# Key matching over four columns in the last three iterations of a graph layer: one wait for four scatters

## The chip, the cores and the metric

One core of a Trainium2 chip runs the whole kernel. The metric is the device time of one execution in microseconds (us), the median over several.

## The reference

Two graph layers in a residual stream over N = 50000 nodes with D = 128 features and E = 25000 edges, sorted by destination. Layer 0 is graph attention. Layer 1, which the change touches, sends a message along each edge and adds it to the row of the edge's source node:

```python
h = jnp.maximum(_layernorm(x, axis=-1), 0.0)
row, col = src, dst                       # edge_index = stack([src, dst])
bond_weights = sigmoid(edge_attr @ Wa + ba)
messages = concatenate([h[row], h[col], edge_attr], axis=-1)
messages = relu(messages @ W1 + b1) @ W2 + b2
messages = messages * bond_weights
x = x + h + segment_sum(messages, row, num_segments=N)
```

## The kernel before

Edges lie in SBUF as 128 partitions by COLS = 196 columns; an edge is a partition and a column. Layer 1 takes G4 = 4 columns in an iteration, so there are ITS = 49 iterations (0 to 48), walked from the last columns to the first. The first four iterations and the last five (44 to 48) are written out, the others are a hardware loop over four at a time; `u` is the iteration modulo 4 and picks one of four buffers.

An iteration runs over four engines, and semaphores alone set the order between them:

- **POOL** issues the indirect transfers: the scatters (L1170), which add a column of 128 message rows to rows of the output in DRAM, and the gathers (L1156) of the source nodes' rows for three iterations ahead (FETCH = 3). An adding scatter reads a row, adds and writes it back, so two scatters that touch the same row must not be in flight together. POOL therefore treats the four columns of an iteration as two pairs: before each pair it waits until all earlier scatters have landed (`ms_add`), and between the pairs it issues gathers. In the last three iterations (46 to 48) there is nothing more to gather. Ahead of the first pair it also waits for the targets (`ms_sx`) and for the message rows UPD (`ms_upd`).
- **PE** transposes the rows of the destination (L1368), those gathered from the source (L1376), the keys (L1357, 128 source indices a column) and the edge features (L1360); multiplies by W1 (L1383, L1385, L1387) and W2 (L1392, L1395); and at last sums rows of equal key with one-hot matrices S2 (L1408). In one pair two edges may have the same source. Their rows are summed, the first of them carries the sum, and the others are sent to spare rows behind the N real ones.
- **DVE** scales the messages by the bond weights (L1269, into MS), and then, in `match`, prepares the next iteration's keys: for each column a compare of the transposed keys of its pair, 256 wide, with its own key, which gives the one-hot matrix S2 (L1250), and a masked count of equal keys that come earlier (L1253, 128 wide for the first and 256 wide for the second column of a pair); then four steps on 128x4 that give the scatter's targets `sx` (L1256 to L1261). Behind it comes `prepare` for three iterations ahead (L1213 to L1230), until iteration 45.
- **ACT** copies out of PSUM: the hidden layer (L1312), UPD (L1326) and the transposed rows (L1306, L1300, L1294).

PE's order in the written-out part of iteration `it` is: W1 of `it+1`, products L1408 of `it`, transposes L1368, L1376, L1357, L1360 of `it+2`, and W2 of `it+1`. Transposes of `it+2` and W1 of `it+1` end with iterations 46 and 47. So L1376 of iteration 48 stands ahead of W2 of iteration 47, and W2 ahead of the scaling and L1408 of iteration 47.

Of the kernel before, what the change touches and what calls it, by code (L numbers as in the profile page):

```python
# [19 lines left out]
ALU = mybir.AluOpType  # L20
# [3 lines left out]
P = 128  # L24
# [11 lines left out]
def gnn_program(nc, x, src, dst, bond, w_embed, a_src, a_dst, w_lin, bias0, w1, b1, w2, b2, wa, ba, out):  # L36
# [27 lines left out]
    with ctx:  # L64
# [103 lines left out]
        with nc.Block() as block:  # L168
# [49 lines left out]
            @block.gpsimd  # L218
            def _(pool):
                nc.gpsimd.memset(ones, 1.0).then_inc(tri_init, 1)  # L220
                pool.wait_ge(tri_init, 1)
                for t, pattern, mult, op in ((ident, [[-1, P]], 1, ALU.is_equal), (ltri[:, P:2 * P], [[-1, P]], 1, ALU.is_gt),
                                             (utri, [[1, P]], -1, ALU.is_gt)):
                    nc.gpsimd.affine_select(out=t[:, 0:P], in_=ones, compare_op=op, fill=0.0, base=0,
                                            pattern=pattern, channel_multiplier=mult).then_inc(consts, 1)
                nc.gpsimd.memset(ltri[:, 0:P], 1.0).then_inc(consts, 1)
                nc.gpsimd.iota(spare[:, :], [[0, 2], [2 * P, 2]], base=2 * N + 1, channel_multiplier=2,
                               allow_small_or_imprecise_dtypes=True).then_inc(consts, 1)
                nc.gpsimd.iota(lane, [[1, COLS]], base=0, channel_multiplier=0,
                               allow_small_or_imprecise_dtypes=True).then_inc(lanes_set, 1)  # L230
                pool.wait_ge(order_known, 1)
                with pool.If(pool.value_load(unsorted[0:1, 0:1]) > 0):
                    lim = pool.to_reg(P * COLS - 1)
                    pool.wait_ge(ranks_ready, 1)
                    pool.wait_ge(ld_unranked, 32)
                    pool.wait_ge(bond_rows, 16)
                    pool.wait_ge(bond_tail, 16)
                    with pool.Fori(0, COLS) as j:
                        nc.gpsimd.tensor_copy(rank1[:, :], rank[:, bass.ds(j, 1)]).then_inc(rank_copied, 1)
                        nc.gpsimd.tensor_copy(pair1[:, :], pairs[:, bass.ds(j, 1), :].rearrange("p o s -> p (o s)")).then_inc(rank_copied, 1)  # L240
                        nc.gpsimd.tensor_copy(bond1[:, :], H[:, bass.ds(j * BOND, BOND)]).then_inc(rank_copied, 1)
                        pool.wait_ge(rank_copied, 3 * j + 3)
                        pool.sem_inc(rank_go, 1)
                        pool.indirect_dma_start(ranked, bass.IndirectOffsetOnAxis(rank1[:, 0:1], 0), pair1[:, :], None,
                                                bounds_check=lim, oob_is_err=True).then_inc(ranked_out, 16)
                        pool.indirect_dma_start(bonds, bass.IndirectOffsetOnAxis(rank1[:, 0:1], 0), bond1[:, :], None,
                                                bounds_check=lim, oob_is_err=True).then_inc(ranked_out, 16)
                        pool.wait_ge(ranked_out, 32 * j + 32)
                        pool.sem_inc(rank_go, 1)
# [880 lines left out]
        cnt, tt, kcol, kdif = (Rw[:, 768 + 4 * n:772 + 4 * n] for n in range(4))  # L1130
        bprod = Rw[:, 1024:1024 + G4 * BOND]
        HDST = Rw[:, 1280:1280 + G4 * D]
        ld_s = [sem(f"ms_gathered{u}") for u in range(4)]
        (ms_keys, ms_bond, ms_flip, ms_hs, ms_bt, ms_hid, ms_hidr, ms_msg, ms_scaled, ms_sum, ms_upd, ms_go, ms_sgo,
         ms_sx, ms_chain, ms_col, ms_zb, ms_bw, ms_fill, ms_hd, ms_flipd, ms_add) = (sem("ms_" + n) for n in (
# [4 lines left out]
        with nc.Block() as block:  # L1140
# [10 lines left out]
            @block.gpsimd  # L1151
            def _(pool):
                lim = pool.to_reg(2 * ROWS_OUT - 1)

                def fetch(u, c):
                    pool.indirect_dma_start(XS4[u][:, c, :], None, halves, bass.IndirectOffsetOnAxis(ixs[:, u, c:c + 1], 0),  # L1156
                                            bounds_check=lim, oob_is_err=False).then_inc(ld_s[u], 16)

                def body(it, u, k):
                    more = upto(it, ITS - 1 - FETCH)  # L1160
                    f = (u + FETCH) % 4
                    for pair in range(2):
                        if pair == 0:
                            pool.wait_ge(ms_sx, it + 1)
                            pool.wait_ge(ms_upd, it + 1)
                        if past(k) or u or pair:
                            pool.wait_ge(ms_add, 32 * (2 * it + pair))  # L1167
                        pool.sem_inc(ms_sgo, 1)
                        for c in (2 * pair, 2 * pair + 1):
                            pool.indirect_dma_start(halves, bass.IndirectOffsetOnAxis(sx[:, u, c:c + 1], 0),  # L1170
                                                    UPD[u][:, c * D:(c + 1) * D], None,
                                                    bounds_check=lim, oob_is_err=True, compute_op=ALU.add).then_inc(ms_add, 16)
                        if more:
                            if pair == 0:
                                pool.wait_ge(ms_ix, it + FETCH + 1)  # L1175
                                if past(k) or u:
                                    pool.wait_ge(ms_flip, it)
                                pool.sem_inc(ms_go, 1)  # L1178
                            fetch(f, 2 * pair)
                            fetch(f, 2 * pair + 1)  # L1180
                for n in range(FETCH):
                    pool.wait_ge(ms_ix, n + 1)
                    for c in range(G4):
                        fetch(n, c)
                loop4(pool, body)
                pool.wait_ge(ms_add, 16 * COLS)

            @block.vector
            def _(dve):
# [42 lines left out]
                def prepare(it, u, k, base):  # L1232
                    fill(it, u, base)
                    weigh(it, u, k, base)

                def match(it, u, early, reused, base):
                    n = [0]

                    def link(ins):
                        n[0] += 1  # L1240
                        ins.then_inc(ms_chain, 1)
                        dve.wait_ge(ms_chain, base + n[0])
                    dve.wait_ge(ms_keys, it + 1)
                    if not early:
                        dve.wait_ge(ms_sum, it - 1)
                    q = blk(it)
                    for c in range(G4):
                        kc = key1[:, bass.ds(q * G4 + c, 1)]
                        p0 = c // 2 * 2 * P
                        nc.vector.tensor_scalar(S2[u % 2][:, c * 2 * P:(c + 1) * 2 * P], bK[u % 2][:, p0:p0 + 2 * P], kc, None, ALU.is_equal)  # L1250
                        w = (1 + c % 2) * P
                        j0 = c // 2 * 3 * P + c % 2 * P
                        nc.vector.scalar_tensor_tensor(junk[:, j0:j0 + w], bK[u % 2][:, p0:p0 + w], kc, ltri[:, 2 * P - w:2 * P],  # L1253
                                                       ALU.is_equal, ALU.mult, accum_out=cnt[:, c:c + 1])
                    k4 = key1[:, bass.ds(q * G4, G4)]
                    link(nc.vector.tensor_tensor(kdif, spare[:, :], k4, ALU.subtract))  # L1256
                    link(nc.vector.tensor_scalar(tt, cnt, 1.0, None, ALU.min))
                    link(nc.vector.tensor_tensor(tt, kdif, tt, ALU.mult))
                    if reused:
                        dve.wait_ge(ms_add, 16 * G4 * (it - 3))  # L1260
                    nc.vector.tensor_tensor(sx[:, u, :], tt, k4, ALU.add).then_inc(ms_sx, 1)  # L1261

                def body(it, u, k):
# [4 lines left out]
                    for c in range(G4):  # L1268
                        last = nc.vector.tensor_scalar(MS[:, c * D:(c + 1) * D], bM[:, c * D:(c + 1) * D], bwc[:, u % 2, c:c + 1],  # L1269
                                                       None, ALU.mult)  # L1270
                    last.then_inc(ms_scaled, 1)
                    if upto(it, ITS - 2):
                        match(it + 1, (u + 1) % 4, not (past(k) or u), past(k) or u == 3, base)
                    if upto(it, ITS - 4):
# [73 lines left out]
            def _(pe):  # L1348
# [50 lines left out]
                def body(it, u, k):  # L1399
# [3 lines left out]
                    if past(k) or u:  # L1403
                        pe.wait_ge(ms_upd, it)
                    pe.wait_ge(ms_sx, it + 1)
                    for c in range(G4):
                        for b in (c // 2 * 2, c // 2 * 2 + 1):
                            last = nc.tensor.matmul(bU[:, c * D:(c + 1) * D], S2[u % 2][:, (2 * b + c % 2) * P:(2 * b + c % 2 + 1) * P],  # L1408
                                                    MS[:, b * D:(b + 1) * D], start=(b % 2 == 0), stop=(b % 2 == 1), skip_group_check=True)
                    last.then_inc(ms_sum, 1)  # L1410
                    if upto(it, ITS - 3):
                        k2 = k + (u >= 2)
# [38 lines left out]
```

## Time and profile before

| what | us |
|---|---|
| median of 3 runs | 1546.91 (1546.25 to 1549.86) |
| the profiled execution, its time | 1547.89 |
| its span, first to last instruction | 1546.1 |
| layer 1's first gather to last scatter issued | 872.5 to 1540.3 |
| an iteration of layer 1 in the loop | about 13.3 |
| iterations 46, 47, 48 on POOL, first scatter | 1507.07, 1519.11, 1531.09 |
| POOL busy, share of the span | 1138.5, 74% |
| mean granted TensorE clock | 0.873 |

The profile gives busy times of each engine, and for an instruction the idle time of its engine just before it with what ended it. A scatter is busy on POOL only while POOL writes its descriptors; the transfer itself goes on behind it, until it lands. The span counts from the first to the last instruction, so the execution's time lies 1.8 us above it.

### The profile page before, as it was taken

Reading aid. Unit: us, or ns where it says so; the run is one execution under the profiler, and the core shown is the slowest. Engines: PE = TensorE matmul, PEld = TensorE weight load, DVE = VectorE, ACT = ScalarE, POOL = GpSimd, SP = SyncE. Lnnn points to the kernel's source line nnn. Section 1 sums busy time; section 2 is a strip of 40 time slices with the busy share of each in tenths; the row PEclk is TensorE's granted clock in tenths of the full one; section 3 lists DMA queues with packets and bytes.
Section 4 is the critical chain, followed back from the end, with each engine's and each line's share of the span. In section 5 each row is a group of like instructions: output and inputs, shape, how many; then the busy total and the mean of one; then the engine's idle time right before and its main releaser. Section 6 shows DMA issues by size and latency. Waiting matters only on the chain. (4 is left out here: it accounts for less than half of the span.)

```text
span 1546.1 us, 26048 instructions
## 1 busy us (share of the span) xinstructions
PE 1014.0 (66%) x5651; PEld 752.9 (49%) x5651; DVE 1102.4 (71%) x3786; ACT 780.6 (50%) x2168; POOL 1138.5 (74%) x992
## 2 busy tenths in 40 slices
PE   0777777777777754555554376777776767676773
PEld 0655555555555534545554154545454444444542
DVE  2989888898988988888889455565565656555551
ACT  0788888888888885656655122222222222222220
POOL 5777777777777704777776568888888888888884
PEclk9989999999999987787777589888898989888897
DMA  8477776777777654555554223333333333333322
GB/s 272 126 216 214 217 226 212 230 210 219 216 215 229 212 172 140 177 174 179 178 172 139 74 41 50 52 49 49 49 51 49 51 49 49 47 50 49 51 40 22
DMA packets 177765, 201.77 MB, mean 131 GB/s; under 512 B 22219, under 2 KB 130767, under 8 KB 177599
## 3 DMA queue, kind: packets, MB, share of 16 engines
q1 hardware_dynamic: 119421, 122.80, 24.8%
q0 software_dynamic: 56496, 71.62, 23.2%
q10 hardware_dynamic: 1810, 6.93, 1.4%
q8 instruction: 13, 0.21, 0.1%
q14 instruction: 25, 0.20, 0.0%
HBM read 90.62 MB, written 109.84 MB: 130 GB/s over the span
## 5 line engine op out<-in xcount | busy, mean ns | idle before, releaser
L1113 POOL DMA_INDIRECT out_dram<-BD,sx x196 | 201.1, 1026 | 118.0 <-issue 63.4
L1156 POOL DMA_INDIRECT XE<-out_dram,ixs x196 | 211.5, 1079 | 70.0 <-issue 53.8
L1269 DVE TENSOR_SCALAR XN<-bank,bwc 128x128 f32<-128x128 f32 x196 | 55.2, 344 | 243.4 <-PE bank L1395 236.0
L710 ACT ACTIVATE BD<-BD,nmr,rstd 128x128 f32<-128x128 f32 x392 | 171.1, 490 | 67.7 <-DVE nmr L571 67.7
L1170 POOL DMA_INDIRECT out_dram<-BS,sx x100 | 160.8, 1608 | 44.2 <-issue 37.9
L1052 PE MATMUL bank<-BD 128*128 128x128 f32 x392 | 105.6, 363 | 119.9 <-DVE BD L933 119.9
L1170 POOL DMA_INDIRECT out_dram<-TS,sx x96 | 153.6, 1600 | 38.1 <-issue 30.2
L1376 PE MATMUL bank<-ident,XE 128*128 128x128 f32 x196 | 42.1, 352 | 184.9 <-DMA XE<-out_dram,ixs 184.9
L773 PE MATMUL bank<-ident,BD 128*128 128x128 f32 x588 | 108.0, 295 | 80.0 <-DVE BD L564 78.9
L785 PE MATMUL bank<-wes,TS 128*128 128x132 f32 x392 | 100.4, 339 | 72.3 <-ACT TS L721 68.9
L1052 PEld LDWEIGHTS bank<-BD 128*128 128x128 f32 x392 | 82.8, 261 | 130.0 <-issue 130.0
L1312 ACT ACTIVATE XN<-bank,b1c 128x512 f32<-128x512 f32 x49 | 33.7, 687 | 207.7 <-PE bank L1387 207.7
L1300 ACT COPY XN<-bank 128x512 f32<-128x512 f32 x49 | 28.7, 586 | 192.6 <-PE bank L1376 192.6
L787 PE MATMUL bank<-wls,TS 128*128 128x128 f32 x784 | 124.8, 284 | 0.0
L435 POOL DMA_INDIRECT XE<-in_x_dram,ix x96 | 100.9, 1051 | 29.3 <-issue 25.9
L1376 PEld LDWEIGHTS bank<-ident,XE 128*128 128x128 f32 x196 | 26.7, 172 | 196.3 <-DMA XE<-out_dram,ixs 196.3
L785 PEld LDWEIGHTS bank<-wes,TS 128*128 128x128 f32 x392 | 60.8, 195 | 118.3 <-ACT TS L721 107.0
L721 ACT ACTIVATE TS<-bank 128x512 f32<-128x512 f32 x196 | 114.4, 584 | 1.4 <-DVE nmr L571 0.7
L773 PEld LDWEIGHTS bank<-ident,BD 128*128 128x128 f32 x588 | 66.6, 147 | 99.2 <-DVE BD L564 93.6
L435 POOL DMA_INDIRECT R<-in_x_dram,ix x88 | 92.0, 1045 | 26.8 <-issue 24.1
L435 POOL DMA_INDIRECT XN<-in_x_dram,ix x88 | 92.0, 1045 | 26.8 <-issue 23.5
L435 POOL DMA_INDIRECT O<-in_x_dram,ix x88 | 91.4, 1039 | 26.8 <-issue 23.5
(229 smaller groups left out, 3236.5 us busy)
## 6 DMA issues: line engine op xcount, KB each, us to landing
out_dram<-BD SPq DMA_DIRECT2D x98, 512.0 KB, 3.0
base_rows<-BD SPq DMA_DIRECT2D x49, 256.0 KB, 3.7
BD<-base_rows SPq DMA_DIRECT2D x49, 256.0 KB, 3.2
H<-BD SPq DMA_DIRECT2D x49, 256.0 KB, 2.8
XE<-in_x_dram SPq DMA_DIRECT2D x13, 512.0 KB
BD<-bond_rows SPq DMA_DIRECT2D x49, 128.0 KB, 2.1
bond_rows<-in_edge_attr_dram ACTq DMA_DIRECT2D x1, 6250.0 KB, 23.9
XN<-in_x_dram SPq DMA_DIRECT2D x12, 512.0 KB, 6.2
```

Of the source, the lines that this page charges most:

```text
L435: pool.indirect_dma_start(XA[u][:, c, SRC - s, :], None, x, bass.IndirectOffsetOnAxis(at, 0), bounds_check=lim, oob_is_err=False).then_inc ...
L710: last = nc.scalar.activation(OT[u][:, g, w:w + D], OT[u][:, g, w + D:w + 2 * D], ACT.Relu, bias=nmr[:, slot, t:t + 1], scale=rstd[:, slot ...
L721: nc.scalar.activation(TS[:, g % 2, :], psT[g % 2][:, :], ACT.Relu).then_inc(ts_ready, 1)
L773: last = nc.tensor.transpose(psT[g % 2][:, q * D:(q + 1) * D], t, ident[:, :])
L785: nc.tensor.matmul(a[:, 0:D + HEADS], t[:, SRC * D:(SRC + 1) * D], wes[:, :], start=True, stop=True, skip_group_check=True)
L787: nc.tensor.matmul(b[:, r * D:(r + 1) * D], t[:, r * D:(r + 1) * D], wls[:, 0:D], start=False, stop=False, skip_group_check=True)
L1052: nc.tensor.matmul(ps[6][:, 0:D], DG[u][:, c, :], BS4[u][:, c, :], start=first, stop=final, skip_group_check=True)
L1113: pool.indirect_dma_start(out, bass.IndirectOffsetOnAxis(sx[:, u, c:c + 1], 0), RO4[u][:, c, :], None, bounds_check=lim, oob_is_err=False) ...
L1156: pool.indirect_dma_start(XS4[u][:, c, :], None, halves, bass.IndirectOffsetOnAxis(ixs[:, u, c:c + 1], 0), bounds_check=lim, oob_is_err=Fa ...
L1170: pool.indirect_dma_start(halves, bass.IndirectOffsetOnAxis(sx[:, u, c:c + 1], 0), UPD[u][:, c * D:(c + 1) * D], None, bounds_check=lim, o ...
L1269: last = nc.vector.tensor_scalar(MS[:, c * D:(c + 1) * D], bM[:, c * D:(c + 1) * D], bwc[:, u % 2, c:c + 1], None, ALU.mult)
L1376: last = nc.tensor.transpose(bS[:, c * D:(c + 1) * D], XS4[u % 4][:, c, :], ident[:, :])
```

## The change

In iterations 46, 47 and 48 (`WIDE` = 46) equal keys are matched over all four columns of the iteration instead of over pairs. Each compare is 512 wide, the counts are 128, 256, 384 and 512 wide, with a mask `upto4` that is put together once in iteration 44. The one-hot matrices S4 and the other buffers lie in columns of H that layer 1 has already used up. L1408 becomes 16 products instead of 8. POOL leaves out the wait ahead of the second pair in these iterations, so that the four scatters follow one wait. The table of spare rows has four different ranges of rows instead of two; it is used in all iterations.

```diff
-                nc.gpsimd.iota(spare[:, :], [[0, 2], [2 * P, 2]], base=2 * N + 1, channel_multiplier=2,
+                nc.gpsimd.iota(spare[:, :], [[2 * P, G4]], base=2 * N + 1, channel_multiplier=2,
...
+        WIDE = ITS - FETCH
+        S4 = [H[:, 8192 + n * 2048:10240 + n * 2048] for n in range(2)]
+        junk4, upto4 = H[:, 12288:14336], H[:, 14336:14336 + G4 * P]
...
-                        if past(k) or u or pair:
+                        wide = isinstance(it, int) and it >= WIDE
+                        if (past(k) or u or pair) and not (wide and pair):
                             pool.wait_ge(ms_add, 32 * (2 * it + pair))
...
+                def wide_keys(it, u):
+                    for c in range(G4):
+                        kc = key1[:, bass.ds(blk(it) * G4 + c, 1)]
+                        w = (1 + c) * P
+                        nc.vector.tensor_scalar(S4[it % 2][:, c * G4 * P:(c + 1) * G4 * P], bK[u % 2][:, :], kc, None, ALU.is_equal)
+                        nc.vector.scalar_tensor_tensor(junk4[:, c * G4 * P:c * G4 * P + w], bK[u % 2][:, 0:w], kc, upto4[:, G4 * P - w:],
+                                                       ALU.is_equal, ALU.mult, accum_out=cnt[:, c:c + 1])
...
+                    if isinstance(it, int) and it >= WIDE:
+                        wide_keys(it, u)
+                    else:
+                        pair_keys(it, u)
...
+                    if isinstance(it, int) and it == WIDE - 2:
+                        nc.vector.tensor_copy(upto4[:, 0:P], ltri[:, 0:P])
+                        nc.vector.tensor_copy(upto4[:, P:2 * P], ltri[:, 0:P])
+                        nc.vector.tensor_copy(upto4[:, 2 * P:4 * P], ltri[:, :])
...
+                    wide = isinstance(it, int) and it >= WIDE
                     for c in range(G4):
-                        for b in (c // 2 * 2, c // 2 * 2 + 1):
-                            last = nc.tensor.matmul(bU[:, c * D:(c + 1) * D], S2[u % 2][:, (2 * b + c % 2) * P:(2 * b + c % 2 + 1) * P],
-                                                    MS[:, b * D:(b + 1) * D], start=(b % 2 == 0), stop=(b % 2 == 1), skip_group_check=True)
+                        for b in range(G4) if wide else (c // 2 * 2, c // 2 * 2 + 1):
+                            hot = S4[it % 2][:, (G4 * b + c) * P:(G4 * b + c + 1) * P] if wide else \
+                                S2[u % 2][:, (2 * b + c % 2) * P:(2 * b + c % 2 + 1) * P]
+                            last = nc.tensor.matmul(bU[:, c * D:(c + 1) * D], hot, MS[:, b * D:(b + 1) * D],
+                                                    start=(b == 0 if wide else b % 2 == 0), stop=(b == G4 - 1 if wide else b % 2 == 1),
+                                                    skip_group_check=True)
```

`pair_keys` holds the compares and counts of before, unchanged.

## Rows read from the trace of the kernel before

**Rows 1.** The chain of waits from 1400 us on, shares by line.
```profile
by line: POOL out_dram L1170 35.1%; issue 28.5%; POOL XE L1156 13.5%; DMA out_dram<-TS,sx 8.9%; DMA out_dram<-BS,sx 6.5%; DMA XE<-out_dram,ixs 1.8%; PE bank L1376 0.5%; POOLq L1178 0.2%; POOLq L1168 0.2%; POOLq L1167 0.1%; POOLq L408 0.1%; 
```

**Rows 2.** The same chain in order of time: start us, us, what.
```profile
1509.00 3.26 DMA out_dram<-TS,sx
...
1514.92 3.30 DMA out_dram<-TS,sx
```

**Rows 3.** POOL's timeline: start us, us, instruction, idle before it and its releaser.
```profile
1505.73 1.03 POOL L1156 DMA_INDIRECT XE<-out_dram,ixs  x1 [0.31 <-issue]
1507.07 1.62 POOL L1170 DMA_INDIRECT out_dram<-TS,sx  x1 [0.30 <-issue]
...
1513.05 1.57 POOL L1170 DMA_INDIRECT out_dram<-TS,sx  x1 [2.49 <-DMA out_dram<-TS,sx]
...
1519.11 1.55 POOL L1170 DMA_INDIRECT out_dram<-TS,sx  x1 [2.62 <-DMA out_dram<-TS,sx]
1520.96 1.55 POOL L1170 DMA_INDIRECT out_dram<-TS,sx  x1 [0.30 <-issue]
...
1526.88 1.55 POOL L1170 DMA_INDIRECT out_dram<-TS,sx  x1 [0.31 <-issue]
1531.09 1.55 POOL L1170 DMA_INDIRECT out_dram<-BS,sx  x1 [2.66 <-DMA out_dram<-TS,sx]
...
1538.77 1.55 POOL L1170 DMA_INDIRECT out_dram<-BS,sx  x1 [0.30 <-issue]
```

**Rows 4.** Landing times of L1170, from 1518 us on, then from 1200 us on.
```profile
DMA to landing us min/median/max: 3.2/3.3/3.4
...
DMA to landing us min/median/max: 3.2/3.3/4.3
```

**Rows 5.** PE's timeline, iterations 46 and 47.
```profile
1502.59 1.95 PE L1408 MATMUL bank<-XN,O 128*128 128x128 f32 x16
1504.38 0.60 PE L1368 MATMUL bank<-ident,BD 128*128 128x128 f32 x4
1508.33 0.66 PE L1376 MATMUL bank<-ident,XE 128*128 128x128 f32 x4 [3.35 <-DMA XE<-out_dram,ixs]
...
1515.63 1.95 PE L1408 MATMUL bank<-XN,O 128*128 128x128 f32 x16
1517.51 0.39 PE L1392 MATMUL bank<-b,on 3*128 3x512 bf16 x1
```

**Rows 6.** ACT's copies of the sums out of PSUM, iterations 47 and 48.
```profile
1517.61 0.58 ACT L1326 COPY TS<-bank 128x512 f32<-128x512 f32 x1 [0.91 <-PE bank L1408]
...
1522.29 0.59 ACT L1326 COPY BS<-bank 128x512 f32<-128x512 f32 x1 [4.09 <-DMA out_dram<-TS,sx]
```

**Rows 7.** Timelines of ACT, POOL and PE, iterations 43 and 44.
```profile
1466.07 0.58 ACT L1326 COPY TS<-bank 128x512 f32<-128x512 f32 x1 [0.91 <-PE bank L1408]
...
1467.66 1.66 POOL L1170 DMA_INDIRECT out_dram<-TS,sx  x1 [0.76 <-issue]
...
1468.51 0.66 PE L1376 MATMUL bank<-ident,XE 128*128 128x128 f32 x4 [2.12 <-DMA XE<-out_dram,ixs]
...
1474.26 1.95 PE L1408 MATMUL bank<-XN,O 128*128 128x128 f32 x16
```

**Rows 8.** PE by stretches: us, busy (count), granted clock, DMA share, GB/s.
```profile
1509.00:1510.50 1.50, 1.50 (x9) 0.59 0.50 44
```

**Rows 9.** DVE's timeline, the scalings of 45 and 48 and match 47.
```profile
1486.58 0.61 DVE L1269 TENSOR_SCALAR XN<-bank,bwc 128x128 f32<-128x128 f32 x2 [7.33 <-PE bank L1395]
...
1501.26 0.34 DVE L1253 SCALAR_TENSOR_TENSOR R<-bank,key,ltri 128x128 f32<-128x128 f32 x1
1501.53 0.48 DVE L1250 TENSOR_SCALAR O<-bank,key 128x256 f32<-128x256 f32 x1
1501.92 0.48 DVE L1253 SCALAR_TENSOR_TENSOR R<-bank,key,ltri 128x256 f32<-128x256 f32 x1
...
1519.02 1.12 DVE L1269 TENSOR_SCALAR XN<-bank,bwc 128x128 f32<-128x128 f32 x4 [1.45 <-PE bank L1395]
```

More of the change, by code:

```diff
@@ L1234, in prepare, with pair_keys @@
                     weigh(it, u, k, base)
+                def wide_keys(it, u):
[5 more added lines that the diff above has]
+                                                       ALU.is_equal, ALU.mult, accum_out=cnt[:, c:c + 1])
+                def pair_keys(it, u):
+                    for c in range(G4):
+                        kc = key1[:, bass.ds(blk(it) * G4 + c, 1)]
+                        p0 = c // 2 * 2 * P
+                        nc.vector.tensor_scalar(S2[u % 2][:, c * 2 * P:(c + 1) * 2 * P], bK[u % 2][:, p0:p0 + 2 * P], kc, None, ALU.is_equal)
+                        w = (1 + c % 2) * P
+                        j0 = c // 2 * 3 * P + c % 2 * P
+                        nc.vector.scalar_tensor_tensor(junk[:, j0:j0 + w], bK[u % 2][:, p0:p0 + w], kc, ltri[:, 2 * P - w:2 * P],
+                                                       ALU.is_equal, ALU.mult, accum_out=cnt[:, c:c + 1])
                 def match(it, u, early, reused, base):
@@ L1245, in match @@
                         dve.wait_ge(ms_sum, it - 1)
+                    if isinstance(it, int) and it >= WIDE:
+                        wide_keys(it, u)
+                    else:
+                        pair_keys(it, u)
                     q = blk(it)
[L1247 to L1254, printed above, removed]
                     k4 = key1[:, bass.ds(q * G4, G4)]
```

## The prediction

> **What bounds the kernel now.** I read the chain of waits of the last 147 us first. Its shares by line say that the layer-1 scatter (L1170) and the gather (L1156), both issued by POOL, carry it, with the scatters' transfers behind them [rows 1]. Up to 1507 us POOL never waits long: it issues scatter, scatter, gather, gather, with 0.30 us between them, and every wait on an earlier scatter is covered by the gathers. From iteration 46 on there is nothing left to gather. In order of time the chain then shows what remains uncovered: 3.26 and 3.30 us from a scatter's issue until it lands, and POOL issues again only about 0.8 us after that [rows 2, 3]. POOL's timeline gives the period exactly. Inside a pair the second scatter starts 1.85 to 1.93 us after the first; between pairs the start moves by 4.05 us in an iteration (1509.00 to 1513.05) and by 4.2 us from one iteration to the next (1526.88 to 1531.09), where POOL passes three waits instead of one [rows 2, 3]. A landing costs 3.2 to 3.4 us in this stretch [rows 4].
>
> So there are five uncovered waits behind the six pairs. The change takes three of them away (inside iterations 46, 47 and 48) and leaves the two between iterations. What has to be asked is what else a group of four waits for, and that is UPD: POOL also waits until ACT has copied the sum out of PSUM (L1326), which follows the one-hot products (L1408) on PE.
>
> **Part 1: three waits go.** Before, the third scatter of an iteration starts about 4.05 us after the second; after, it starts 1.87 us after it. This gives 4.05 - 1.87 = 2.18 us each, 6.5 us in all, if POOL alone set the pace. That is the most that the change can give.
>
> **Part 2: the products double.** L1408 now multiplies four blocks into each of four columns, 16 products for 8; PE shows each as two matmuls, so x32 for x16. From the start of L1408 to the next work on PE are 1504.38 - 1502.59 = 1.79 us for the x16 at full clock [rows 5]; the second x16 adds as much. Nearer zero would need PE to have had room in those 1.79 us, but the matmuls stand back to back; at half clock it would be up to 3.6 us, and this is the upper bound. I take 1.79. The path here is PE, ACT's copy, POOL, so it counts in full wherever UPD is awaited.
>
> How long from the copy to POOL: in iteration 43 the copy ends at 1466.07 + 0.58 = 1466.65 and POOL, idle before, starts at 1467.66, 1.01 us later [rows 7]. In iteration 47 of before the copy ends at 1517.61 + 0.58 = 1518.19 [rows 6] and POOL starts at 1519.11 [rows 3], 0.92 us later. So there the copy and the landing (1514.92 + 4.2 = 1519.1, rows 2) allow the same start: iteration 47 has no slack for its UPD already. That is the place where the gain is lost.
>
> **Iteration 46.** Its copy starts 1.98 us after L1408 (1517.61 - 1515.63, rows 5 and 6), so 1502.59 + 1.98 + 1.79 = 1506.36; end 1506.94, POOL at 1507.95 for 1507.07. The four scatters start at 1507.95, 1509.88, 1511.75 and 1513.62, and by the landing alone iteration 47 could start at 1513.62 + 4.19 = 1517.8.
>
> **Iteration 47.** Its messages hang on the last gather, issued at 1505.73, before any scatter that moves, and landed at 1508.33, when PE goes on (L1376) [rows 3, 5]. The products of iteration 46 and the transposes L1368 behind them now end at 1504.98 + 1.79 = 1506.8 and are still out of the way. But PE then idles 1.6 us before L1376 where it idled 3.35. In before the granted clock falls to half at about 1509.3, after these 3.35 us (0.59 is the mean of 1509.00 to 1510.50) [rows 8], and L1376 to L1408 takes 1515.63 - 1508.33 = 7.30 us [rows 5]. In iteration 44, after an idle stretch of 2.12 us, the same work ran faster: 1474.26 - 1468.51 = 5.75 us [rows 7]. With 1.6 us idle I take 5.75, the value of the row with the shorter idling, and 7.30 as the bound. Then L1408 starts at 1514.08, the copy at 1514.08 + 1.98 + 1.79 = 1517.85, ends 1518.43, and POOL starts at 1519.44. This is later than the landing allows (1517.8) and 0.3 us later than before: all that iteration 46 saved is lost here.
>
> A rule of the Trainium skill bears on this ("TensorE: Matmul & The Clock Gate", Part 1: The HAM clock gate): the gate's default is the slow state, activity releases it, and the point at which it switches differs from run to run for one kernel. By the trace, the stretch after 2.12 us of idling runs in its shorter time, and the sum is the one above; by the page's remark on runs a fall could still come at another place, and the sum would be that of the second rival.
>
> **Iterations 47 and 48.** Four scatters: 1519.44 + 3 x 1.85 = 1525.0; landing and waits 4.21: iteration 48 starts at 1529.2 for 1531.09. UPD of 48 is in time: L1392 follows L1408 of 47 at 1.88 + 1.79 = 3.67 after its start, the scaling (L1269) 1.51 later (1519.02 - 1517.51) [rows 5, 9], at 1519.3; from it to the copy 3.27 us before (1522.29 - 1519.02) [rows 6, 9], 5.06 now, so the copy ends at 1524.9 and POOL could start at 1525.9, 3.3 us before it is asked. The last scatter of all starts at 1529.2 + 5.55 = 1534.8 for 1538.77: **4.0 us** earlier. Nothing behind it changes.
>
> **Part 3: DVE.** Steps of DVE from start to start: 0.27 us for 128 columns (1501.26 to 1501.53), 0.39 for 256 (1501.53 to 1501.92) [rows 9], so some 0.13 for each further 128. Wide: four compares of 512 (0.65 each) and counts of 128, 256, 384 and 512 (0.27, 0.39, 0.52, 0.65), 4.43 us; before 6 x 0.39 + 2 x 0.27 = 2.88. So 1.55 us more in each of three matches (nothing as the lower bound, 2.9 if all doubled). It is covered: match 48 ended 1.45 us before the last scaling, that is 1.94 after the start of L1408 of 47; now at 3.49, and the scaling comes at 5.18: slack 1.7. Match 47, running at 1501 and now over by about 1506.1, is due at L1408 of 47, 1514.1, and match 46 as long before its own. If the cover were gone, each us late in match 48 would first use up that 1.7 and the 3.3 of UPD 48. The three copies of masks in iteration 44, 128x128 twice and 128x256 once, cost between nothing and 0.27 + 0.27 + 0.39 = 0.93 us by the same steps; DVE idles 7.33 us before the next scaling, at 1486.58 [rows 9], so nothing.
>
> **Part 4: the table of spare rows** now differs over four columns in all iterations. Only which rows the few duplicates go to changes; instruction and bytes stay: nothing.
>
> **The sum.** 4.0 us off this execution's own 1547.9 (span 1546.1, 1.8 around it) gives 1543.9; the median of the runs shown is 1546.91, 1.0 lower, and the prediction is made against that: **1542.9 us**, 0.26% less. The measurement tells about 0.3%, 4.6 us, from nothing, so this lands just inside "no change".
>
> **Rivals.**
> - *Nothing takes over.* POOL alone sets the pace, UPD 47 is in time: 6.5 us, 1540.4. It needs UPD 47 some 2.5 us earlier than worked out. For it only the bound; against it the row in which copy and landing already tie. 0.10.
> - *The clock falls again* in the stretch before UPD 47. Then 7.30 for 5.75: start of 47 at 1521.0, gain 2.4, 1544.5. For it the row of before; against it the shorter idling. 0.15.
> - *The fourth scatter lands later* since four read-modify-write transfers follow one another: the loop shows landings up to 4.3 us [rows 4]. One us more, in 47 and in 48, leaves 2.0: 1544.9. Against it: at most two are in flight at a spacing of 1.87 us and 3.3 us each, as in a pair now. 0.10.
> - *The other side, slower*: the same mechanism grown to a queue. X us more per landing cost 2X, and X - 1.6 more once iteration 46's slack (1519.4 - 1517.8) is gone. From 1.9 us more (5.2 for 3.3) nothing is gained; from 3.4 more (6.7) it is slower by 0.3%, about 1551.5. No landing in the tail is over 3.4. 0.03.
> - The forecast: 0.62. It spreads by about 1 us for the measurement and for 0.86 to 1.01 us from copy to POOL.
>
> **How the numbers follow.** The range goes from the first rival's 1540.4 to 1545.6, past the third's 1544.9 by what the runs scatter; about 0.15 is left out. Within the forecast somewhat more than a third lies beyond 4.6 us: 0.62 x 0.38 = 0.24, with the first rival 0.10: faster 0.34. Slower 0.03. Same 0.63. The first kernel's runs reach up to 1549.86, which says that single ones can be 3 us off.
>
> **What would show it.** After: in iterations 46 to 48 L1170 x4 with 0.30 us between; POOL's wait before 47 put down to ACT or PE, or a landing that was over 1.5 us before; L1408 x32 in 3.7 us; L1376 to L1408 in about 5.75 us at clock 1.00; UPD 48 ready 3 us early; the last scatter about 5.55 us after the first of 48. I am wrong if POOL's wait before 47 is 2.6 us again (then 46 was worth its 2 us), if the clock shows 0.5 before 1512, or if landings exceed 3.4.

## The result and the profile after

The changed kernel takes 1545.26 us (median of 22 runs, 1541.37 to 1548.92); the first kernel beside it 1547.89 (22 runs, 1541.81 to 1552.44). The ratio is 0.9982, with a 95% interval of 0.9974 to 0.9991: 2.8 us faster, between 1.4 and 4.0. Forecast were 4.0 us less and a time of 1542.9. The interval lies wholly below 1, so the change makes the kernel faster, by less than the 0.3% that the prediction called "no change". The measured time lies 2.4 us above the forecast one: 1.0 of them because the first kernel itself has a median of 1547.89 here and had 1546.91 in the three runs that the forecast started from, 1.4 because the gain between the medians is 2.6 us and not 4.0.

POOL's timeline of the changed kernel (start us, us, instruction, idle before it and its releaser; L1160 is the gather, L1175 the scatter) answers to [rows 3]:

```profile
1506.99 1.04 POOL L1160 DMA_INDIRECT XE<-out_dram,ixs  x1 [0.30 <-issue]
1508.88 1.62 POOL L1175 DMA_INDIRECT out_dram<-TS,sx  x1 [0.84 <-ACT TS L1349]
1510.81 1.57 POOL L1175 DMA_INDIRECT out_dram<-TS,sx  x1 [0.31 <-issue]
1512.68 1.57 POOL L1175 DMA_INDIRECT out_dram<-TS,sx  x1 [0.31 <-issue]
1514.56 1.56 POOL L1175 DMA_INDIRECT out_dram<-TS,sx  x1 [0.30 <-issue]
1520.56 1.55 POOL L1175 DMA_INDIRECT out_dram<-TS,sx  x1 [4.44 <-ACT TS L1349]
...
1526.14 1.55 POOL L1175 DMA_INDIRECT out_dram<-TS,sx  x1 [0.30 <-issue]
1530.36 1.55 POOL L1175 DMA_INDIRECT out_dram<-BS,sx  x1 [2.66 <-DMA out_dram<-TS,sx]
...
1535.93 1.55 POOL L1175 DMA_INDIRECT out_dram<-BS,sx  x1 [0.30 <-issue]
```

The waits inside the iterations are gone. But the wait ahead of iteration 47 has grown from 2.62 us to 4.44, and its releaser is no longer a transfer but ACT's copy of UPD.

The last gather of this execution comes 1.26 us later than in the trace of before (1506.99 for 1505.73); the scatter of the stretch ahead of it is shown at the end of the section on the prediction. So I count from there: **G is the start of the last gather**, and everything the change touches on the path lies behind it. Times after G, in us:

| start of | before | predicted | after |
|---|---|---|---|
| iteration 46 | 1.34 | 2.22 | 1.89 |
| iteration 47 | 13.38 | 13.71 | 13.57 |
| iteration 48 | 25.36 | 23.5 | 23.37 |
| the last scatter | 33.04 | 29.1 | 28.94 |

The tail is 4.1 us shorter, forecast 4.0. PE and ACT in the same stretch (L1399 the transposes of the gathered rows, L1434 the products, L1349 the copy into UPD) answer to [rows 5, 6]:

```profile
1503.67 3.73 PE L1434 MATMUL bank<-XN,H 128*128 128x128 f32 x32
1507.44 0.59 ACT L1349 COPY TS<-bank 128x512 f32<-128x512 f32 x1 [2.70 <-PE bank L1434]
1509.67 0.66 PE L1399 MATMUL bank<-ident,XE 128*128 128x128 f32 x4 [1.83 <-DMA XE<-out_dram,ixs]
1515.41 3.73 PE L1434 MATMUL bank<-XN,H 128*128 128x128 f32 x32
1519.18 0.59 ACT L1349 COPY TS<-bank 128x512 f32<-128x512 f32 x1 [2.70 <-PE bank L1434]
1525.64 0.59 ACT L1349 COPY BS<-bank 128x512 f32<-128x512 f32 x1 [5.88 <-DMA out_dram<-TS,sx]
```

The products take 3.73 us for 1.95, 1.78 more. PE idles 1.83 us before L1399 instead of 3.35, and from L1399 to L1434 are 5.74 us instead of 7.30. The stretches view of PE (us, busy, granted clock, DMA share, GB/s) shows the difference, and answers to [rows 8]:

```profile
1509.50:1511.00 1.50, 1.33 (x12) 1.00 0.00 0
1511.00:1512.50 1.50, 1.50 (x12) 1.00 0.52 44
1512.50:1514.00 1.50, 1.50 (x5) 1.00 0.50 44
```

The granted clock is 1.00, the level of 2.4 GHz, in all three stretches; in [rows 8] the mean was 0.59. The chain of waits in order of time shows the new path, from the last gather over PE and ACT to iteration 47:

```profile
1506.99 2.63 DMA XE<-out_dram,ixs
1509.67 0.66 PE bank L1399 x4
...
1515.58 3.58 PE bank L1434 x32
1519.18 0.59 ACT TS L1349
1519.81 0.76 issue
...
1526.14 3.33 DMA out_dram<-TS,sx
```

In [rows 1] PE had 0.5% of the chain from 1400 us on; the same view of the changed kernel gives its lines over 6%.

### The profile page after: what moved, and what is told of

Read it like the earlier page. It is cut to its first block and busy times, and to the rows that moved or that the text cites. A ratio compares the mean times of both kernels' runs of the same rounds, so it can differ in the third digit from the quotient of the medians.

```text
span 1543.3 us, 26147 instructions
## 1 busy us (share of the span) xinstructions
PE 1021.3 (66%) x5699; PEld 760.3 (49%) x5699; DVE 1107.9 (72%) x3789; ACT 781.3 (51%) x2168; POOL 1138.5 (74%) x992
## 5 line engine op out<-in xcount | busy, mean ns | idle before, releaser
L1160 POOL DMA_INDIRECT XE<-out_dram,ixs x196 | 211.7, 1080 | 69.8 <-issue 57.6
L1175 POOL DMA_INDIRECT out_dram<-BS,sx x100 | 160.7, 1607 | 43.6 <-issue 39.7
L1175 POOL DMA_INDIRECT out_dram<-TS,sx x96 | 153.6, 1600 | 35.2 <-issue 29.6
L1399 PE MATMUL bank<-ident,XE 128*128 128x128 f32 x196 | 41.4, 347 | 182.7 <-DMA XE<-out_dram,ixs 182.7
L1399 PEld LDWEIGHTS bank<-ident,XE 128*128 128x128 f32 x196 | 26.4, 170 | 194.0 <-DMA XE<-out_dram,ixs 194.0
L435 POOL DMA_INDIRECT XN<-in_x_dram,ix x88 | 91.9, 1044 | 26.8 <-issue 23.5
L435 POOL DMA_INDIRECT O<-in_x_dram,ix x88 | 91.4, 1039 | 26.8 <-issue 23.5
```

The costliest lines, as they stand in the source:

```text
L435: pool.indirect_dma_start(XA[u][:, c, SRC - s, :], None, x, bass.IndirectOffsetOnAxis(at, 0), bounds_check=lim, oob_is_err=False).then_inc ...
L1399: last = nc.tensor.transpose(bS[:, c * D:(c + 1) * D], XS4[u % 4][:, c, :], ident[:, :])
```

## The experiments

The theory: of the three waits, the one in iteration 46 is worth nothing, since iteration 47 starts when UPD 47 is there; the doubled products delay that; the waits in 47 and 48 are worth their 2.2 us each, less what the start of 47 loses. The rival: the start of 47 hangs on the transfers, or the change costs something elsewhere. All tails below are read as above, from G to the start of the last scatter, each from one trace. Two traces of the changed kernel agree in it to 0.1 us (28.94 and 28.89).

Experiments 1 and 2 and the first runs of 3 and 4 were made on a chip on which the first kernel takes 1744.44 us (median of 35 runs). No trace of the first kernel was taken there, but with only the table changed the tail is 33.11 us, for 33.04. The second runs of 4 and experiments 5 and 6 have 1546.88 us beside them, the second run of 3 and experiments 7, 8 and 9 have 1548.36 (medians of 23 runs of the first kernel). Experiments 5 to 8 are one execution each, of 1545.5 to 1546.4 us: single times scatter by more than what they are to tell apart, so only their tails are used.

**1. Only the table of spare rows.**
```diff
-                nc.gpsimd.iota(spare[:, :], [[0, 2], [2 * P, 2]], base=2 * N + 1, channel_multiplier=2,
+                nc.gpsimd.iota(spare[:, :], [[2 * P, G4]], base=2 * N + 1, channel_multiplier=2,
```


> The first kernel with only the new table of spare rows. Measured in the trace from the start of the last gather (G) to the start of the last scatter: 33.04 us in the first kernel, 28.94 us in the changed one. Theory (the table costs nothing, and the 1.3 us by which the changed kernel's last gather comes later is scatter of runs): 33.0 us after G, ratio of times 1.000. Rival (the table's other spare rows slow the transfers or something ahead of layer 1): ratio about 1.001, G about 1.2 us later than in the first kernel.

Tail 33.11 us, ratio 0.9994 (0.9979 to 1.0009): the table costs nothing in the tail, and nothing that the times can tell.

**2. Wide matching, but with the waits.**
```diff
-                        if (past(k) or u or pair) and not (wide and pair):
+                        if past(k) or u or pair:
                             pool.wait_ge(ms_add, 32 * (2 * it + pair))
```


> The changed kernel with the wait ahead of the second pair put back in iterations 46 to 48, so that only the cost of wide matching is left. Theory (the products delay UPD by 1.8 us, which shows where UPD is awaited): iteration 46 starts at G + 1.9 us for 1.34, iteration 47 is then set by the landing at G + 13.9, iteration 48 at G + 25.9, the last scatter at G + 33.6: 0.55 us slower than the first kernel, ratio 1.0004. Rival (wide matching costs nothing on the path): G + 33.0. Rival (DVE's longer match counts too): G + 35 or more.

Iterations 46, 47 and 48 start at G + 2.04, 14.22 and 26.21, the last scatter at 34.00; ratio 1.0010 (1.0000 to 1.0021). The cost of wide matching alone is 0.9 us in the tail, more than the 0.55 expected. Most of it comes from the start of 46, which is 0.7 us later; the starts of 47 and 48 are 0.8 and 0.9 later, and the last scatter 0.9 beside experiment 1:

```profile
1703.30 1.04 POOL L1160 DMA_INDIRECT XE<-out_dram,ixs  x1 [0.30 <-issue]
1705.34 1.62 POOL L1175 DMA_INDIRECT out_dram<-TS,sx  x1 [1.00 <-issue]
...
1717.52 1.55 POOL L1175 DMA_INDIRECT out_dram<-TS,sx  x1 [2.68 <-DMA out_dram<-TS,sx]
```

It is POOL's timeline of that kernel. The 2 us or more of the rival in which DVE's longer match counts do not appear.

**3. Wide only in iterations 47 and 48** (twice).
```diff
-        WIDE = ITS - FETCH
+        WIDE = ITS - 2
```


> Wide only in iterations 47 and 48. Theory (iteration 46's saved wait is worth nothing, since UPD 47 sets the start of 47): iteration 46 at G + 1.34, its PE idles 3.35 us before L1376 as in the first kernel. If the clock keeps its full level in the stretch behind that, iteration 47 starts at G + 13.7 and the last scatter at G + 29.0, as good as with three; if it falls as in the first kernel's trace, 15.3 and 30.6. Rival (each wait taken away is worth its 2.18 us): the last scatter at G + 31.1 or 28.9 + 2.2.

> Wide in 47 and 48 once more. PE idles about 3.4 us ahead of the transposes of the gathered rows. Theory (whether the clock falls behind this is luck of the run): L1399 to L1434 takes 5.75 us at full clock or 7.3 with a fall, iteration 47 starts at G + 13.7 or 15.1, the last scatter at G + 29.0 or 30.4. Over the runs the ratio lies at 0.9978 (3.4 of 1547 us), between the change's and one with 2.7 us. Rival: ratio 0.997, as the first time, which the tail cannot explain.

Iteration 47 starts at G + 15.11 and in the second run at 15.19, the last scatter at 30.42 and 30.49. In both traces PE idled 3.6 us before L1399 and its clock then fell. The second one's stretches:

```profile
1509.00:1510.50 1.50, 1.40 (x8) 0.66 0.45 38
1510.50:1512.00 1.50, 1.50 (x7) 0.50 0.26 14
1512.00:1513.50 1.50, 1.50 (x10) 0.71 0.32 35
```

L1399 to L1434 takes 7.31 us in both, and the start of 47 (15.1) is the one expected for a fallen clock. So the tail is 2.6 us shorter than before. The ratio was 0.9971 both times (0.9958 and 0.9959 to 0.9983), 5.1 and 4.5 us: more than the tail accounts for (the intervals begin at 3.0 and 2.6), and the rival of the second expectation is right on that number. More on it below.

**4. UPD in halves** (twice, the second time beside the changed kernel). In iterations 47 and 48 the sums of columns 2 and 3 go to a PSUM bank that is free by then, ACT copies columns 0 and 1 as soon as they are summed, and POOL waits for the other half only ahead of the third scatter (`halved(it)` is `it >= WIDE + 1`).
```diff
+                            if halved(it):
+                                pool.wait_ge(ms_updh, it - WIDE)
...
+                        elif halved(it):
+                            pool.wait_ge(ms_upd, it + 1)
...
+                        act.wait_ge(ms_half, it - WIDE)
...
+                        nc.scalar.copy(UPD[u][:, 0:2 * D], bU[:, 0:2 * D]).then_inc(ms_updh, 1)
+                        act.wait_ge(ms_sum, it + 1)
+                        nc.scalar.copy(UPD[u][:, 2 * D:4 * D], bD[:, 2 * D:4 * D]).then_inc(ms_upd, 1)
```


> The changed kernel, but in iterations 47 and 48 the sum of columns 2 and 3 goes to another PSUM bank, ACT copies columns 0 and 1 as soon as they are summed, and POOL waits for the second half only ahead of the third scatter. Theory (the second half of the products is what delays the start of 47): 47 starts at G + 11.8 for 13.57, where the landing of 46 and the half copy tie; the last scatter at G + 27.1 for 28.94; 5.9 us off the first kernel's tail, ratio about 0.9963. Rival (the start of 47 is set by the transfers): 47 at G + 13.5 and the last at G + 28.9, ratio as the change's 0.998.

> The changed kernel itself beside the next one. Theory: tail from G to the last scatter 28.9 us if PE keeps its full clock behind the last gather, ratio 0.9976 (4.1 of about 1744 us) within the scatter. Rival (the change costs 1 to 1.5 us ahead of the tail as well): ratio 0.9984.

> The kernel with half copies once more, beside the changed kernel on one chip. Theory: the tail is 1.8 us shorter than the changed kernel's (27.1 us from G), so the median is 1.8 us lower within the scatter of about 1 us, ratio to the first kernel 0.9966. Rival (something that the tail does not show takes the 1.8 us back): no difference between the two medians.

Iteration 47 starts at G + 11.79 and 12.09, the last scatter at 27.10 and 27.42, 5.9 and 5.6 us before the first kernel's. The changed kernel beside the second run: 13.59 and 28.89, as in its first trace. ACT's timeline of the second run, iteration 47 (L1359 copies the first half, L1361 the second):

```profile
1515.40 0.37 ACT L1359 COPY TS<-bank 128x256 f32<-128x256 f32 x1 [0.91 <-PE bank L1451]
1517.19 0.37 ACT L1361 COPY TS<-bank 128x256 f32<-128x256 f32 x1 [1.41 <-PE bank L1451]
```

and POOL, the fourth scatter of 46 and the first of 47:

```profile
1512.86 1.56 POOL L1185 DMA_INDIRECT out_dram<-TS,sx  x1 [0.30 <-issue]
1517.12 1.55 POOL L1185 DMA_INDIRECT out_dram<-TS,sx  x1 [2.70 <-DVE sx L1290]
```

The first half is there at 1515.77, 1.35 us before POOL starts, so now the landing sets the start: 4.26 us after the fourth scatter, as between iterations before. The releaser that the view names is not the right one. This write of `sx` ended just before, at 1516.96, but it holds the targets of iteration 48, and POOL waits at 47 only for those of 47, which were written at 1505.52. In the first run the view names the landing, 4.10 us after the fourth scatter:

```profile
1712.37 1.55 POOL L1185 DMA_INDIRECT out_dram<-TS,sx  x1 [2.54 <-DMA out_dram<-TS,sx]
```

Times: 0.9985 (0.9972 to 0.9998) on the first chip, 0.9971 (0.9959 to 0.9982) beside the changed kernel's 0.9979 (0.9968 to 0.9990) on the second; medians 1541.77 and 1543.63, for 1546.88. The 1.86 us between the two medians are the 1.8 expected, and drawing the twelve times of each kernel anew many times leaves 0.5 to 3.4 us between them. On the first chip the expected 0.9963 did not come: it lies outside the interval, and the median there (1740.63) is no lower than that of experiment 3 (1740.41), whose tail is 3.3 us longer. It is the fastest of the kernels by its tail.

**5. The products of iteration 47 twice.** The sums are the same; the second round starts anew.
```diff
-                    for c in range(G4):
+                    for c in [*range(G4)] * (2 if isinstance(it, int) and it == ITS - 2 else 1):
```


> The changed kernel with the 16 products of iteration 47 multiplied twice (the sums are the same), which adds about 3.6 us on PE there. G is the start of the last gather. Theory (the start of iteration 47 hangs on PE through UPD): it moves with the whole addition, from G + 13.6 to G + 17.1, and the last scatter from G + 28.9 to G + 32.5. Rival (the landing of iteration 46 sets it): nothing moves up to the first 1.6 us, or at all.

L1434 takes 7.31 us, and POOL's wait before 47 is:
```profile
1511.71 1.56 POOL L1175 DMA_INDIRECT out_dram<-TS,sx  x1 [0.31 <-issue]
1521.05 1.55 POOL L1175 DMA_INDIRECT out_dram<-TS,sx  x1 [7.78 <-ACT TS L1349]
```
With G at 1503.89 the start of 47 is at G + 17.16 (expected 17.1), the last scatter at G + 32.53 (32.5). Every us on PE there is a us of the tail.

**6. The products of iteration 48 twice.** The same edit with `it == ITS - 1`.

> The changed kernel with the 16 products of iteration 48 multiplied twice, 3.6 us more on PE. Theory (UPD 48 is ready about 3.1 us before the landing of 47 lets iteration 48 start): nearly all of it is covered, iteration 48 starts at G + 23.8 for 23.4 and the last scatter at G + 29.4 for 28.9. Rival (PE counts in each wide iteration): the last scatter at G + 32.5.

The copy of UPD 48 starts at 1529.20, with G at 1506.91, which is 3.6 us later after G than in the changed kernel, and POOL:
```profile
1526.11 1.55 POOL L1175 DMA_INDIRECT out_dram<-TS,sx  x1 [0.30 <-issue]
1530.58 1.55 POOL L1175 DMA_INDIRECT out_dram<-BS,sx  x1 [2.91 <-ACT BS L1349]
```
Iteration 48 starts at G + 23.67, the last scatter at 29.24: of 3.6 us more, 0.3 show. The slack of UPD 48 is therefore about 3.3 us, the number of the prediction.

**7. The products of iteration 46 twice.** The same edit with `it == ITS - 3`.

> The changed kernel with the 16 products of iteration 46 multiplied twice. Theory: UPD 46 comes 3.6 us later, iteration 46 starts at G + 5.5 for 1.9, its landing then sets 47 at G + 15.3 for 13.6 (iteration 46 has about 1.8 us of slack, the rest counts; PE reaches L1399, the transpose of the gathered rows, 1.5 us late, which would give 15.1), the last scatter at G + 30.6 for 28.9. Rival (46 counts in full): G + 32.5.

The last scatter is at G + 28.76, so nothing at all is lost, less than I had expected. Here L1434 of 46 began at 1502.75, 5.25 us before G (1508.00), and in the changed kernel's trace 3.32 before it (1503.67 and 1506.99), so iteration 46 started at 3.52 and not at 5.5. Its landing allowed G + 13.4 (9.20 + 4.2), and PE set it at 13.47. Iteration 46 has slack in the changed kernel, and its size goes with when PE gets there.

**8. Wide only in iteration 48**, `WIDE = ITS - 1`.

> Wide only in iteration 48. Theory (UPD 48 has 3 us of slack, so this one wait is worth its whole 2.18 us, and 47 starts as in the first kernel): iteration 47 at G + 13.4, 48 at G + 25.4, the last scatter at G + 30.9. Rival (each wide iteration pays 1.8 us on PE): the last scatter at G + 32.7.

Last scatter at G + 31.92, expected 30.9. From the start of 48 to the last scatter are 5.58 us for 7.68 before, 2.1 less: the wait is worth what was expected. What is missing is ahead of it: PE idled 4.99 us before L1399, and its granted clock was 0.50 from there to 1512,

```profile
1507.71 1.11 PE L1399 MATMUL bank<-ident,XE 128*128 128x128 f32 x4 [4.99 <-DMA XE<-out_dram,ixs]
...
1515.95 1.95 PE L1434 MATMUL bank<-XN,O 128*128 128x128 f32 x16
```

that is 8.24 us from L1399 to L1434, and iteration 47, with narrow products as in the first kernel, started at G + 14.28 for 13.38. UPD 47 can thus set the start even without wide products, when the clock is low.

**9. Wide in 47 and 48, and the eight products of 46 twice**: more work on PE ahead of the gathered rows. Beside the edit of experiment 3:
```diff
-                    for c in range(G4):
+                    for c in [*range(G4)] * (2 if isinstance(it, int) and it == WIDE - 1 else 1):
```


> Wide in 47 and 48, and the eight products of iteration 46 multiplied twice, so that PE idles 1.6 us instead of 3.4 (more work, the same sums). Theory (a busy PE keeps its clock): L1399 to L1434 takes 5.75 us, UPD 47 allows G + 13.6, but iteration 46 now starts at 2.1 and its landing sets 47 at G + 14.2; the last scatter at G + 29.5, less than the 30.4 of the kernel with less work when its clock falls. Rival (the clock has nothing to do with the idling before): 7.3 us from L1399 to L1434 in some of the looks here too, 47 at G + 15.1.

PE idled 0.56 us before L1399, and the clock stayed:

```profile
1509.00:1510.50 1.50, 1.21 (x11) 1.00 0.00 0
1510.50:1512.00 1.50, 1.50 (x12) 1.00 0.05 2
1512.00:1513.50 1.50, 1.50 (x6) 1.00 0.45 41
```

L1399 to L1434 takes 5.74 us where experiment 3 took 7.31, so UPD 47 would have allowed about G + 13.6. But the products of 46 were late in this run (G - 2.05), iteration 46 started at 3.15 and its landing set 47 at 15.21. Last scatter at G + 30.61, expected 29.5, ratio 0.9981 (0.9969 to 0.9993): the clock was won, and the gain lost again to the start of 46.

Put together, by the idling of PE ahead of the transposes of the gathered rows of iteration 48:

| traces | idle, us | L1399 to L1434, us |
|---|---|---|
| wide in 46, or its products twice (9 traces) | 0 to 1.83 | 5.74 in all |
| spare table only | 3.36 | 5.74 |
| before; experiment 3, twice | 3.35, 3.61, 3.62 | 7.30, 7.31, 7.31 |
| experiment 8 | 4.99 | 8.24 |

## Why the prediction was right

**The direction and the place** were right. 4.0 us were predicted for the tail and 4.1 came, at the places named: nothing from iteration 46, 0.2 us later (0.3 predicted) at the start of 47, then 2.2 and 2.1. Experiments 5, 6 and 7 show by doubled products, one trace each, that PE sets the start of 47 in full, that of 48 only beyond 3.3 us, and that of 46 without effect on the end. Experiment 4 hands the first half over early, and the tail falls by 1.8 and 1.5 us, for the 1.8 of the products' second half. Of the signs that the prediction names, all came but one: it would be wrong if landings exceeded 3.4 us, and in iteration 46 the first took 3.5 and the third 4.8. No wait hung on them.

The prediction read from the trace of before that iteration 47 has no slack for its UPD. That holds where the clock falls. In experiment 1, whose kernel differs in the table alone, it did not fall, and the copy ended 2.50 us before POOL started (1713.84 and 1716.34), 1.5 us or more earlier than needed; iteration 47 started at G + 13.41 all the same, by the landing.

**Part 1**, 2.18 us for a wait: 2.1 in experiment 8, its one trace. **Part 2**, 1.79 us for eight more products: 1.78. **The copy to POOL**: 1.01 us were taken from iteration 43, 0.79 (1520.56 - 1519.77) were measured at 47 and 0.85 at 46; this makes 47 0.2 us earlier, and as PE went on after the last gather 0.1 later than taken (2.68 for 2.60 us after G), 47 came 0.14 us before the forecast; at 46 it is half of the 0.3. **Part 3**, DVE: match 48 runs from 1513.69 to 1518.95 in the changed kernel and the scaling waits for PE 1.64 us more (1.7 predicted); covered. **Part 4**: nothing, by experiment 1.

**The clock** was the step least certain: 5.75 us taken, 7.30 as the bound, and 5.74 came. The tails say that it held in each of the nine traces in which PE idled at most 1.8 us, and fell in four of the five in which it idled 3.3 us or more. Behind each of the iterations' gathers from the fourth on PE has this stretch, from the transposes of the gathered rows to the one-hot products. In PE's timelines of all fourteen traces there are 644, and 643 of them begin with an idle wait:

| idle before the stretch, us | stretches | of these in 5.7 us | the others, us |
|---|---|---|---|
| under 3.0 | 130 | 129 | 7.3 |
| 3.0 to 4.0 | 302 | 68 | 7.2 to 7.3 |
| 4.0 and more | 211 | 0 | 7.0 to 8.6 |

Where the stretches view was asked, 5.7 us go with a clock of 1.00 and 7.3 with one that was at 0.50 for a part. So the 1.6 us of idling that the prediction worked out were on the safe side of this table, and the 3.35 of before lie where both happen. This fits what the Trainium skill says under "TensorE: Matmul & The Clock Gate", Part 1: The HAM clock gate, that activity releases the gate and that the switching point differs between runs: at 3.35 and 3.36 us of idling one run fell and the other did not. Experiment 9, which changed only how busy PE is before, shows it most directly, in one trace. In the changed kernel the doubled products of iteration 46 thus cost 1.8 us where POOL has that much slack, and go with a clock worth 1.5 us where POOL waits. Where POOL has no such slack, in experiments 2 and 4, they cost 0.7 to 0.8 us.

**The rivals.** "Nothing takes over" would have given a tail of 26.5; with halves it is 27.1 to 27.4. The rest is the start of iteration 46, 0.7 and 0.8 us later than before in these two traces, which counts as soon as the landing of 46 sets the start of 47. "The fourth scatter lands later": it does not, 3.3 to 3.4 us for each fourth scatter of the changed kernel's trace.

**The size of the whole** was off: 4.0 us predicted for the time, 2.8 measured, in the second comparison 3.2 (0.9979), while the tail says 4.1 in both. The step that lacks a term is "1.8 us around the span", taken for both kernels. In every recorded run of the first kernel and of experiment 1 the time lies 1.66 to 1.88 us above the span, and in every run of every kernel that is wide in any iteration 2.01 to 2.13. These 0.3 us are outside the first and last instruction, so no part of the tail shows them; the table does not cause them, and what does is not shown. They leave 3.8 of the 4.1 us, which the interval of 1.4 to 4.0 holds.

They do not explain the others. Less 0.3 us, the tails give 2.3 us for experiment 3, where 5.1 and 4.5 were measured and the intervals begin at 3.0 and 2.6. For the halves they give 5.6 and 5.3, where 2.6 and 4.5 were measured: outside the first interval (0.3 to 4.9) and inside the second (2.8 to 6.3). What makes these differences is not shown. What the traces show is that the stretch ahead of the tail is not constant. From the first gather to the first scatter of layer 1 pass 26.0 us in before, 26.4 in the changed kernel and 22.3 in its second trace, the same code; from there to G pass 607.2, 607.3 and 609.4. Over the fourteen traces the two together take 630.6 to 634.9 us, with the two narrow kernels inside this (633.2 and 631.3), and from the last scatter to the end pass 7.3 to 7.5 us in all. One execution thus scatters by 4 us ahead of the tail, and single traces cannot say whether the averages of the kernels differ there. This stays open.

**The chances.** For a gain above 4.6 us the prediction gives 0.38 within a forecast of 4.0 that spreads "by about 1 us". A bell curve with a standard deviation of 1 us gives 0.27; 0.38 needs one of 2 us. The single times do scatter by 2 us, but a median of 22 does so by less.

## What to carry to other kernels

When a wait is taken off an engine, look for the second thing that the next step waits for and how much later it ends: here two releasers ended together in the trace of before, and the one of them that the change makes 1.8 us longer took the first of three savings away. If the freed step then waits for a result that comes in parts, hand it over in parts: copying UPD in halves gave back 1.5 to 1.8 us of what the wider products had cost. And for a change of a few us at the end of a long kernel, count from the last event that the change can't move; whole times scatter by 2 us and more.

## What the runs showed of the hardware

Two executions of one kernel, in two measurements, differed by 4 us in the first 26 us of layer 1, through the point at which the TensorE clock rises from 0.5 to 1.00 while a dependent chain runs on PE; of this the next 600 us, paced by POOL, gave back 2.1 us. PE by stretches, the changed kernel's first trace and then its second, each 3 us ahead of and behind the moment 12.3 us after the first gather:

```profile
882.70:885.70 3.00, 3.00 (x4) 0.50 0.25 61
885.70:888.70 3.00, 2.76 (x5) 0.50 0.18 48
```

```profile
884.90:887.90 3.00, 3.00 (x6) 0.83 0.23 63
887.90:890.90 3.00, 2.54 (x21) 1.00 0.16 46
```

The second has its full clock while the first still works at half. Four adding scatters 1.86 us apart land as pairs do, 3.2 to 3.5 us after each issue, with one of twelve at 4.8. From the end of ACT's copy to POOL's next scatter pass 0.79 to 1.01 us, and 0.30 from one transfer on POOL to the next where nothing is awaited. And the kernel takes 1744 us on one chip and 1547 on another, with the same tail to 0.1 us (experiment 1 and before): what differs lies ahead of layer 1, whose first gather is at 1071.6 us there for 872.5.
